# Causal attention: projections, values and joins as pairs of 64-column products, spread over three PSUM banks, in a new order

## What is computed

```python
xn = _layernorm(x)
qkv = jnp.einsum('bse,ehd->bshd', xn, qkv_w) + qkv_b          # 16 heads of 64
q, k, v = jnp.split(qkv, 3, axis=-1)
logits = jnp.einsum('bqhd,bkhd->bhqk', q, k) / sqrt(64)
probs = softmax(where(tril, logits, large_negative))
attn = jnp.einsum('bhqk,bkhd->bqhd', probs, v)
x = x + jnp.einsum('bqhd,hde->bqe', attn, out_w) + out_b + ffn(xn)
```

## Time and profile before

| What | us |
|---|---|
| median of 3 runs (1464.54 to 1470.5) | 1467.65 |
| the profiled execution | 1468.25 |
| its span, first to last instruction | 1466.5 |
| PE busy | 1414.2 (96%) |
| DVE busy | 1254.1 (86%) |
| ACT busy | 917.8 (63%) |
| POOL busy | 970.4 (66%) |

### The profile page before, as it was taken

One profiled execution on the slowest core, in us unless ns is written; L12 is line 12 of the kernel. 1 busy time (PEld: TensorE's weight loads), 2 busy tenths in 40 slices (PEclk: granted clock), 3 DMA queues, 4 the chain that ended last, 5 costly groups with the idle time before them and its releaser, 6 DMA issues.

```text
span 1466.5 us, 27229 instructions
## 1 busy us (share of the span) xinstructions
PE 1414.2 (96%) x9282; PEld 905.1 (62%) x9282; DVE 1254.1 (86%) x1966; ACT 917.8 (63%) x1862; POOL 970.4 (66%) x756
## 2 busy tenths in 40 slices
PE   8989999999999999999999998789999999999998
PEld 7756555555565565655655555456667676776767
DVE  7588888888888888888888877399999999999997
ACT  3456666766676666666666675557665675657552
POOL 5145545546555556555556554559999999999895
PEclk9999999999999999999999999999999999999999
DMA  8058777877787777777787778300000000000000
GB/s 191 1 130 213 180 175 174 194 169 177 174 190 182 173 176 187 172 185 178 180 190 170 171 182 202 86 1 1 1 8 8 1 8 1 8 8 1 8 1 15
DMA packets 77140, 163.98 MB, mean 112 GB/s; under 512 B 31410, under 2 KB 43724, under 8 KB 77004
## 3 DMA queue, kind: packets, MB, share of 16 engines
q1 hardware_dynamic: 77004, 162.24, 46.5%
HBM read 9.08 MB, written 2.10 MB: 8 GB/s over the span
## 4 chain that ended last, share of the span: by engine, by line
PE 83%; DVE 7%; issue 4%; POOL 3%; ACT 2%; DVEq 0%; ACTq 0%; POOLq 0%
PE accum L1096 18%; PE both L1031 13%; PE misc L998 9%; PE both L2786 8%; PE flips_all L1031 6%; PE flips_all L2809 4%; PE flips_all L1120 4%; PE misc L1008 4%; PE flips_all L2798 3%; PE flips_all L2846 2%; PE accum L2798 2%; PE accum L2809 2%; PE flips_all L2832 1%; ACT big L534 1%; PE flips_all L969 1%
## 5 line engine op out<-in xcount | busy, mean ns | idle before, releaser
L453 POOL TENSOR_SCALAR big<-big,recip 128x384 f32<-128x384 f32 (+7 forms) x512 | 376.1, 749 | 414.8 <-DVE recip L705 414.8
L713 DVE STREAM_TRANSPOSE big<-big 128x896 f32<-128x896 f32 (+7 forms) x288 | 346.0, 1228 | 17.5 <-POOL big L453 17.2
L534 ACT ACTIVATE big<-both,neg_max 128x1024 f32<-128x1024 f32 (+3 forms) x256 | 243.3, 956 | 169.0 <-DVE neg_max L695 160.5
L1096 PE MATMUL accum<-across,v_sb 128*64 128x256 f32 (+1 forms) x2560 | 271.6, 363 | 11.0 <-issue 10.9
L1096 PEld LDWEIGHTS accum<-across,v_sb 128*64 128x64 f32 x2560 | 178.8, 137 | 132.7 <-issue 68.9
L695 DVE TENSOR_REDUCE neg_max<-both 128x1 f32<-128x1024 f32 (+3 forms) x256 | 248.3, 1011 | 7.8 <-PE both L1036 7.8
L1031 PE MATMUL both<-qk_sb 64*128 64x512 f32 (+3 forms) x1024 | 212.9, 532 | 12.5 <-issue 8.6
L2786 PE MATMUL both<-slow_sb,h_T 128*128 128x512 f32 x384 | 181.1, 599 | 7.9 <-DVE xnT L2299 4.4
L1595 POOL TENSOR_TENSOR prod<-xnT,qs 128x1024 f32<-128x1024 f32 (+3 forms) x32 | 180.2, 5635 | 11.1 <-DVE qs L2299 11.1
L534 ACT ACTIVATE big<-flips_all,neg_max 128x128 f32<-128x128 f32 (+3 forms) x256 | 131.9, 526 | 83.3 <-DVE neg_max L695 46.9
L1031 PEld LDWEIGHTS both<-qk_sb 64*128 64x128 f32 x1024 | 93.9, 186 | 117.5 <-issue 117.5
(11 more groups left out here) (224 smaller groups left out, 2403.7 us busy)
## 6 DMA issues: line engine op xcount, KB each, us to landing
across<-big SPq DMA_DIRECT2D x1024, 144.0 KB, 2.5
out<-x SPq DMA_DIRECT2D x8, 256.0 KB, 2.3
x<-in_L_attn_x SPq DMA_DIRECT2D x3, 512.0 KB, 5.6
slow_sb<-in_L_attn_w_slow SPq DMA_DIRECT2D x3, 512.0 KB, 7.2
w_qk<-in_L_attn_qkv_w SPq DMA_DIRECT2D x2, 512.0 KB, 6.5
xn<-in_L_ffn_W SPq DMA_DIRECT2D x1, 1024.0 KB
x<-in_L_attn_x SPq DMA_DIRECT2D x2, 256.0 KB, 3.0
qs<-in_L_attn_qkv_w SPq DMA_DIRECT2D x1, 512.0 KB, 6.1
```

What stands on the lines that cost most here:

```text
L453: pool.tensor_scalar(part, part, recip[:, u % 2, SLOTS.index(row), h:h + 1], 0.0, ALU.mult, ALU.add).then_inc(scaled, 1)
L534: last = act.activation(probs_of(row, h).rearrange("p b j k -> p j b k"), scores_of(row, h).rearrange("p (j b k) -> p j b k", b=MOVES, k=3 ...
L713: dve.transpose(part, part).then_inc(turned[group_of(row)], 1)
L1096: last = pe.matmul(dst, lhsT=values_of(u, j, h), rhs=keys_of(g, rows[n:n + 2], j, h), start=j == 0, stop=j == rows[n + 1])
```

## The change

Projections, values and joins are each computed as two products of 64 columns, h = 0 into partitions 0 to 63 and h = 1 into partitions 64 to 127 of the same bank, where one full product stood. Values 1 and the projections (0, 1) and (0, 0) go through banks 1, 0 and 1, which the small scores and joins use too; only unit 0's six, and two transposes at the end, still use bank 2 alone. `weigh` takes a list of (first row of a pair, from, to) and is cut into four parts at other places.

PE's body becomes: score 0, values 1, project (1, 1), weigh group 0 (keys 0 and 1), small 4, score 1, weigh group 0 (keys 2 and 3 of rows 6, 7), project (0, 1), project (0, 0), weigh group 0 (the rest), small 6, score 2, project (1, 0), weigh group 1 (rows 2, 3), small 5, values 0, score 3, weigh group 1 (rows 4, 5), join 0, join 1. The lists of DVE, ACT and POOL change their order too. SP issues the same moves in the same order, but at the other end of its body, so that the loads of the expert weights, which stand in bodies 2 and 31, come ahead of another move. The diff, cut: the tables of the orders (`Tally`), the join (changed as the projections are) and the lines in layer 1 that finish the last unit in the new order are left out.

```diff
+LAST_LOW = 0, 0
-BANK = {('v', 0): 2, ('qk', 0, 1): 2, ('qk', 1, 0): 2, ('qk', 0, 0): 2, ('qk', 1, 1): 2, ('o', 0): 0, ('o', 1): 1, ('v', 1): 2}
+BANK = {('v', 1): 1, ('qk', 1, 1): 2, ('qk', 0, 1): 0, ('qk', 0, 0): 1, ('qk', 1, 0): 2, ('v', 0): 2, ('o', 0): 0, ('o', 1): 1}
+FIRST = ('v', 0), ('qk', 0, 1), ('qk', 1, 0), ('qk', 0, 0), ('qk', 1, 1), ('v', 1)
...
+            k = 2 if u in (0, UNITS) and key in FIRST else BANK[key]
+            return k, uses_at[k](u, *key)
...
+                move(u - 1, 0)
                 move(u - 1, 1)
-                move(u, 0)
...
@@ GpSimd, unit(u)
                 scale(u, 7, 0)
+                scale(u, 7, 1)
                 scale(u, 0, 1)
                 scale(u, 1, 0)
-                scale(u, 7, 1)
+                scale(u, 1, 1)
                 scale(u, 0, 0)
-                scale(u, 1, 1)
...
+                scale(u, 5, 0)
                 scale(u, 5, 1)
-                scale(u, 5, 0)
...
@@ ScalarE, softmax
-                elif row == STEP_ROWS[step][-1]:
+                elif row == (LAST_LOW[h] if step == SMALL else STEP_ROWS[step][-1]):
                     last.then_inc(bank_kept[h], 1)
...
@@ ScalarE, unit(u)
+                keep_values(u + 1, 1)
+                softmax(u, 7, 0)
                 softmax(u, 7, 1)
-                softmax(u, 7, 0)
                 if UNITS - B <= u < UNITS - 1:
                     first_norms(u - (UNITS - B))
+                keep_part(u + 1, 1, 1)
+                softmax(u, 1, 0)
+                softmax(u, 1, 1)
+                softmax(u, 0, 0)
                 softmax(u, 0, 1)
-                softmax(u, 0, 0)
-                softmax(u, 1, 1)
-                softmax(u, 1, 0)
-                keep_values(u + 1, 0)
+                softmax(u, 6, 1)
+                keep_part(u + 1, 0, 1)
+                keep_part(u + 1, 0, 0)
                 softmax(u, 6, 0)
-                keep_part(u + 1, 0, 1)
-                softmax(u, 6, 1)
+                keep_att(u - 1, 0)
+                softmax(u, 2, 0)
+                softmax(u, 2, 1)
                 keep_part(u + 1, 1, 0)
-                keep_att(u - 1, 0)
-                softmax(u, 2, 1)
-                softmax(u, 2, 0)
                 softmax(u, 5, 0)
                 softmax(u, 5, 1)
-                keep_part(u + 1, 0, 0)
-                keep_att(u - 1, 1)
+                softmax(u, 3, 1)
                 softmax(u, 3, 0)
-                softmax(u, 3, 1)
-                keep_part(u + 1, 1, 1)
+                keep_values(u + 1, 0)
                 softmax(u, 4, 0)
                 softmax(u, 4, 1)
-                keep_values(u + 1, 1)
+                keep_att(u - 1, 1)
                 keep_join(u - 1, 0)
                 keep_join(u - 1, 1)
...
@@ VectorE, unit(u)
+                maximum(u - 1, 7, 0)
                 maximum(u - 1, 7, 1)
-                maximum(u - 1, 7, 0)
+                maximum(u - 1, 1)
                 maximum(u - 1, 0)
-                maximum(u - 1, 1)
                 invert(u - 1, 0)
-                invert(u - 1, 4)
+                maximum(u - 1, 6, 1)
                 maximum(u - 1, 6, 0)
-                maximum(u - 1, 6, 1)
...
+                invert(u - 1, 4)
                 turn(u - 1, 7)
+                turn(u - 1, 0)
                 invert(u - 1, 1)
+                turn(u - 1, 1)
                 maximum(u - 1, 2)
-                turn(u - 1, 0)
-                turn(u - 1, 1)
                 turn(u - 1, 6, 0)
                 turn(u - 1, 6, 1)
-                invert(u - 1, 6)
                 maximum(u - 1, 5, 0)
                 maximum(u - 1, 5, 1)
...
+                invert(u - 1, 6)
+                maximum(u - 1, 3)
+                invert(u - 1, 2)
                 turn(u - 1, 2)
-                invert(u - 1, 2)
-                maximum(u - 1, 3)
                 maximum(u - 1, 4, 0)
                 maximum(u - 1, 4, 1)
...
@@ TensorE, project
-                pe.matmul(pool_of[k], lhsT=w_qk[:, c, P * n:P * (n + 1)], rhs=xnT[:, u // PAIRS, 512 * half:512 * (half + 1)],
-                          start=True, stop=True).then_inc(bank_made[k], 1)
+                for h in range(2):
+                    at = P * n + D * h
+                    last = pe.matmul(pool_of[k][D * h:D * (h + 1), :], lhsT=w_qk[:, c, at:at + D],
+                                     rhs=xnT[:, u // PAIRS, 512 * half:512 * (half + 1)], start=True, stop=True)
+                last.then_inc(bank_made[k], 1)
...
@@ TensorE, project_values
-                    last = pe.matmul(pool_of[k][:, 256 * r:256 * (r + 1)], lhsT=xnT[:, b, P * (2 * c + r):P * (2 * c + r + 1)],
-                                     rhs=w_v[:, P * n:P * (n + 2)], start=True, stop=True)
+                    for h in range(2):
+                        at = P * (2 * c + r) + D * h
+                        last = pe.matmul(pool_of[k][D * h:D * (h + 1), 256 * r:256 * (r + 1)], lhsT=xnT[:, b, at:at + D],
+                                         rhs=w_v[:, P * n:P * (n + 2)], start=True, stop=True)
...
@@ TensorE, unit(u)
                 score(u, 0)
+                project_values(u + 1, 1)
+                project(u + 1, 1, 1)
+                weigh(u - 1, 0, (0, 0, 2), (2, 0, 2))
                 score_small(u, 4)
-                project_values(u + 1, 0)
-                weigh(u - 1, 0, 0, 4)
                 score(u, 1)
...
+                weigh(u - 1, 0, (2, 2, 4))
+                project(u + 1, 0, 1)
+                project(u + 1, 0, 0)
+                weigh(u - 1, 0, (2, 4, 8))
                 score_small(u, 6)
-                project(u + 1, 0, 1)
-                weigh(u - 1, 0, 4, 8)
-                project(u + 1, 1, 0)
                 score(u, 2)
...
-                project(u + 1, 0, 0)
-                weigh(u - 1, 1, 0, 4)
-                weigh(u - 1, 1, 4, 6)
+                project(u + 1, 1, 0)
+                weigh(u - 1, 1, (0, 0, 4))
                 score_small(u, 5)
+                project_values(u + 1, 0)
                 score(u, 3)
-                project(u + 1, 1, 1)
+                weigh(u - 1, 1, (2, 0, 6))
                 join(u - 1, 0)
                 join(u - 1, 1)
-                project_values(u + 1, 1)
```

More of the change, by code:

```diff
@@ L122, with __init__ @@
 GROUPS = (0, 1)
-EARLY = (('qk', 0, 1), ('qk', 1, 0))
+EARLY = (('qk', 1, 1), ('qk', 0, 0))
 class Tally:
[L128 to L132, removed]
+    def __init__(self, order, head=None, tail=None, over=()):
+        self.at, n = {}, 0
+        for body in range(-1, UNITS + 2):
+            if body == -1 and head is not None:
+                keys = [(key, 1) for key in head]
+            elif body >= UNITS and tail is not None:
+                keys = [(key, -1) for key in tail]
+            else:
+                keys = order
+            for key, ahead in keys:
+                if 0 <= body + ahead < UNITS:
                     n += 1
                     self.at[(body + ahead,) + key] = n
-        self.met = 0
+            for key in over if body == UNITS - 1 else ():
+                n += 1
+                self.at[(UNITS,) + key] = n
+        self.met, self.total = 0, n
     def __call__(self, u, *key):
@@ L208, in layer0 @@
                 ((0,), -1), ((1,), -1),
-            ])
+            ], tail=((0,), (1,)))
     tails = {}
@@ L1088, in weigh @@
                     has_values(u, 0)
-                if hi > GB:
+                if parts[-1][2] > GB:
                     has_values(u, 1)
-                for n in range(0, GB, 2):
-                    for j in range(lo, min(hi, rows[n + 1] + 1)):
+                for n, lo, hi in parts:
+                    for j in range(lo, hi):
                         own = int(j > rows[n])
@@ L1097, in weigh @@
                                              start=j == 0, stop=j == rows[n + 1])
-                if hi > rows[3]:
+                if parts[-1][0] == 2 and parts[-1][2] > rows[3]:
                     weighed_at.meet(u, "high", g)
@@ L1119, in join @@
                 for r in range(GB):
-                    last = pe.matmul(pool_of[k][:, P * r:P * (r + 1)], lhsT=att_T[:, g, P * r:P * (r + 1)], rhs=outw_sb[:, u % PAIRS, :],
-                                     start=True, stop=True)
+                    for h in range(2):
+                        at = P * r + D * h
+                        last = pe.matmul(pool_of[k][D * h:D * (h + 1), P * r:P * (r + 1)], lhsT=att_T[:, g, at:at + D],
+                                         rhs=outw_sb[:, u % PAIRS, :], start=True, stop=True)
                 last.then_inc(bank_made[k], 1)
@@ L1196, in layer0 @@
         first_over = ones_made, u_cleared, score_cleared, earlier_made
-        last_k = BANK[("v", 0)]
         return (first_over, [[(weighed, weighed_at(UNITS - 1, "high", g)) for g in range(2)], [(moved[g], 16 * MOVES * MOVES * UNITS) for g in range(2)], (added, 2 * UNITS)], (bank_kept[2], uses_at[2](UNITS, *EARLY[1])),
-                (scores_ready, UNITS * len(scores_at.order)),
```

(10 more changed lines are left out.)

59 lines of the change are left out of this document (27 added, 32 removed).

## The result

The changed kernel takes 1460.87 us, the median of 6 runs (1456.26 to 1462.32), against 1467.65: a ratio of 0.9946 (95% interval 0.9925 to 0.9966). Timed once more beside other kernels it gave 1458.89 us (1457.26 to 1459.89), where the kernel before gave 1468.89: a ratio of 0.9936 (0.9923 to 0.9949). So it is faster by 7 to 10 us; 21 us were forecast. The direction was right and the time lies in the range, but only a third to a half of the gain came. The profiled execution took 1462.21 us, its span 1460.4, so it is read against 1468.25 and 1466.5.

A forecast was written before the change was run, and what follows sets the result against it. TensorE was taken to bound layer 0's bodies: work 25.37 us plus waits 0.5 gives 25.87, 0.75 less. 31 x 0.75 = 23, less 2 for the loads, is 21: 1468.25 - 21 = 1447 us, range 1427 to 1464.

The forecast's parts named there:

- PE's work: TensorE's work in one layer-0 body, without waits: from 26.03 us to 25.37.
- W, for the move: Layer-0 body: weighing's first part (group 0) waits for SyncE's move of the body before; 0.1 us.
- J1, for ACT's copy: End of a layer-0 body: the second join waits for ScalarE's copy of weighing's second group; 0.3 us.
- the rest of the old waits: Layer-0 bodies: of 0.32 us of old waits, spread over single bodies, 0.1 is kept.
- That just fits; I put 0.1 on it.: Group 0's move on SyncE lands 28.4 to 29.3 us after its body starts; weighing wants it at 29.6.
- Rival 2: Layer 0: waits give the gain back; row 6 turned 1.3 us later, body 26.4, total 1464 us; chance 0.16.
- the expert loads, at +2: Bodies 2 and 31: 1 MB loads ahead of another move cost 2 us once for both, from 0 to 4.
- the row form: Layer-0 scores stand in five runs instead of four: one entry more, 0.17 us more per body.
- the pairs with their joints: Projections, values, joins in weighing's form: 0.93 us less per body, plus 0.10 for eight joints inside the new runs.
- projections at 0.88 in a run: Sign in layer-0 bodies: a projection inside a run takes 0.86 to 0.9 us instead of 1.06.
- S1 without a wait: Layer-0 body: row 6's score no longer waits for the exponentials of row 7's score; 0.27 us gone.
- pairs that run side by side: Layer 0: 64-column pairs overlap; the rival that they don't costs 6.9 us a body, 1680 us, chance 0.01.

## Why the prediction failed

| per body | forecast | measured |
|---|---|---|
| PE's work | 25.37 | 25.49 (fastest bodies, and the median without the full moves) |
| W, for the move | 0.1 | 0.44 (4.21 - 3.77) |
| J1, for ACT's copy | 0.3 | under 0.05 (0.8 us in 3 waits) |
| the rest of the old waits | 0.1 | 0.11 (25.60 - 25.49) |
| body | 25.87 | 26.08, with body 1 26.11 |

Body 0 was forecast at the same 0.75 less and took 3.1 more; start and end were forecast at +2 together and took 2.8 + 3.1 = 5.9 more. So the 15 us between the forecast and the profiled execution are 30 x 0.24 = 7 in the bodies, and 3.9 + 3.9 = 8 at the ends.

*The step that failed is "That just fits; I put 0.1 on it."* in the paragraph on SyncE's moves. The loop was written out rightly, and each of its parts was in the forecast: S1 at 6.4 (measured 6.4 in the kernel with the short moves, where W does not wait), the move 10.0 behind it, 12.0 to 12.9 long, wanted at 3.7 in the next body (3.77). But 10.0 was one body's value, where the mean was already 10.21 and became 10.37; and 12.9, read from one move of group 1 (494.36 to 507.25), was taken as the far end of a move of group 0, where it became the mean. Those are 0.4 and 0.5 us on a sum that had 0.75 to spare in the middle of its range, against a period that the forecast itself had shortened to 25.87. The runs with longer, shorter and shared moves show that this wait is what remains. Rival 2, the loop as the bound, had the mechanism, from a cause that was not needed (row 6 turned 1.3 late; it is 0.16 later), and its kind of price: one issue (10.05 / 16 = 0.63 us) more cost 0.42 a body, one fewer gave 0.32.

*The ends were mis-sized*: the forecast costed the expert loads, at +2, and nothing else. It moved s4 behind V, P and W to give S1 its time, and did not ask what stands there in body 0, where no W exists: PE is idle for 1.9 us more in it. In the setup the pairs stand between full products, where they add changes of form instead of saving them (1.8 us). Some 6 of the 9 us go with stretches at half the clock (1.7 in the setup, 1.6 in body 0 and 3.1 behind the last S0, each an estimate from the granted clock); the forecast had no term for the clock, and why it fell more often than before stays open.

*J1's wait* did not come: the three waits are 0.3 at most. The Trainium skill's PSUM Bottleneck (TensorEngine Tiling (Array Packing), Performance Considerations) says that the copies out of PSUM may become the bottleneck after a speedup by tiling. The trace does not show that here: ACT is 64% busy, and the joins start right behind W. The forecast's error of 0.3 was in the other direction and hid most of the one on the move.

*Nearly right were* PE's terms. In the fastest bodies, from block to block, the scores take 9.68 where they took 9.56: +0.12 for the row form (forecast +0.17). All the rest takes 15.82 where it took 16.48: -0.66 for the pairs with their joints (forecast -0.93 + 0.10 = -0.83). Together these two make the 0.12 by which PE's work missed. The dear run is W J J: 4.50 (486.92 to 491.42) against 4.09 of arithmetic at 0.86 per 512 columns, so 0.42 over, where the other runs are 0.15 to 0.31 over. With full products it takes 4.54, though it then has one change of form more, so the joins' pairs brought next to nothing in the new order. The number of products alone is not the reason: in the old order the last P, the joins and V take 3.94 either way (487.05 to 490.99, and 487.81 to 491.75 with pairs). What makes this run dear is open. Right too were projections at 0.88 in a run, S1 without a wait, and pairs that run side by side.

What stays open: why the moves take 0.56 us longer than before with the same 16 DMAs and the same data. From the first issue to the last it is 10.15 for 9.83, and from the last issue to its landing 2.76 for 2.53.

## What to carry to other kernels

Before a faster engine's gain is counted, write out each loop that runs through little of its work, with means and spread over many bodies, and compare the sum with the *new* period: a slack of 0.75 us with a jitter of 2 is no slack. An order that hides a wait behind the work of the unit before has a price in the first body, where that work is missing: 1.9 us here. And look at the ends with their granted clock: all that was lost ahead of body 1 and behind the last S0 came to 9 of the 15 us that the bodies gained, most of it at half the clock, and it is not shown that the change made the clock fall. When a transfer bounds the loop, one issue on another engine's queue at an idle place can be worth more than all that the new order and form had brought; a second one beside it cost it all.

## What the hardware showed

A DMA issued by ACT took 0.52 us of its queue, and two behind each other 1.42 in most bodies (mean 1.49), so that the second took 0.9; on SP 16 take 10.05 us in the move shown, 0.63 each. A full product of 128 x 128 and two products of 64 columns side by side run at the same rate in 32-bit (0.86 to 0.88 us per 512 columns), so I read the pairs' gain as that of the changes of form: 0.68 us for five in the new order, 0.79 for four in the old, on average 0.14 to 0.20 for each that goes. Behind gaps of 2.3 to 4.0 us PE worked at half its clock (granted 0.50) for 2.4 to 3.4 us in the changed kernel's profile, so that such a gap can cost more than its length: S1 at 75.23 took 1.57 us longer than in the steady state. But behind the same gap of 2.44 a second profile kept the full clock.
